# Graph transformer layer, gate logits: full 32-bit products on 32-column weights in place of two-part products on 128 columns

## The reference, cut to what matters

```python
x = x + gnn(xn, ...) + mix(xn, ...)            # attention parts
z = _layernorm(x, axis=-1)                     # (12500, 256)
all_out = _experts_mlp(z, eW1, eb1, eW2, eb2, eW3, eb3)   # 4 experts
shared  = _shared_mlp(z, sW1, sb1, sW2, sb2, sW3, sb3)
gates   = softmax(z @ gW + gb)                 # gW is (256, 4)
topv, topi = top_k(gates, 2)
topw    = softmax(topv)
out     = x + shared + sum(sel(all_out, topi) * topw)
```

## Time and profile before

| what | value |
|---|---|
| median of 3 runs | 1440.02 us (1438.76 to 1440.14) |
| the profiled execution | 1439.86 us, of which the span of the trace is 1438.1 us |
| mean granted TensorE clock | 0.984 |
| PE busy | 1382.2 us (96%) |
| PEld busy | 1244.2 us (87%) |
| DVE busy | 1053.4 us (73%) |
| ACT busy | 769.6 us (54%) |
| POOL busy | 954.6 us (66%) |
| DMA | 121.81 MB, mean 85 GB/s |

### The profile page before, as it was taken

How to read it: one execution, slowest core, us unless ns; L and a number is a source line. 1 busy time by engine, 2 the same in 40 slices (tenths; PEclk the granted TensorE clock), 3 DMA queues, 4 the chain that set the end, 5 groups by cost and what they waited for, 6 DMA issues and landing times.

```text
span 1438.1 us, 26970 instructions
## 1 busy us (share of the span) xinstructions
PE 1382.2 (96%) x9032; PEld 1244.2 (87%) x9032; DVE 1053.4 (73%) x2566; ACT 769.6 (54%) x1339; POOL 954.6 (66%) x873
## 2 busy tenths in 40 slices
PE   5999999679999999999999999999999999999987
PEld 5999999567888888988889888888888888888875
DVE  6877778657777777777778777777777777777761
ACT  4555556125654556545665456554565555655553
POOL 5776766367666776667766677666776666776352
PEclk9999999899999999999999999999999999999998
DMA  5777767222212222121220212202122121220000
GB/s 180 253 261 251 227 207 240 59 66 59 66 30 66 58 72 67 27 65 58 72 68 25 67 55 72 68 25 68 54 72 70 28 64 54 72 72 22 15 15 14
DMA packets 71630, 121.81 MB, mean 85 GB/s; under 512 B 38053, under 2 KB 42786, under 8 KB 71598
## 3 DMA queue, kind: packets, MB, share of 16 engines
q1 hardware_dynamic: 55598, 108.00, 23.6%
q0 software_dynamic: 16000, 13.43, 4.3%
HBM read 69.47 MB, written 51.70 MB: 84 GB/s over the span
## 4 chain that ended last, share of the span: by engine, by line
PE 91%; DVE 3%; POOL 2%; issue 1%; ACT 1%; DVEq 1%; POOLq 1%; DMA 0%; SPq 0%; ACTq 0%
PE psum L224 27%; PE psum L225 26%; PE psum L226 26%; PE psum L421 4%; PE psum L642 1%; PE psum L494 1%; PE psum L573 1%; PE psum L572 1%; PE psum L690 1%; PE psum L566 1%; PE psum L625 1%; PE psum L664 1%; POOL xg L1350 1%; POOL ag L1352 1%; DMA attn_bc<-in_L_gnn_attn_l 0%
## 5 line engine op out<-in xcount | busy, mean ns | idle before, releaser
L224 PE MATMUL psum<-w_hi,h_hi 128*125 128x256 f32 x600 | 171.6, 286 | 4.9 <-DVE h_lo L1236 3.7
L226 PE MATMUL psum<-w_hi,h_lo 128*125 128x256 f32 x600 | 169.3, 282 | 0.0
L225 PE MATMUL psum<-w_lo,h_hi 128*125 128x256 f32 x600 | 169.2, 282 | 0.0
L1350 POOL DMA_INDIRECT xg<-table_xt,idx x100 | 124.6, 1246 | 55.7 <-issue 55.7
L1356 POOL TENSOR_TENSOR h_lo<-relu,h_hi 128x1000 fp32r<-128x1000 f32 x50 | 127.3, 2568 | 29.0 <-ACT h_hi L792 29.0
L1154 DVE SCALAR_TENSOR_TENSOR base<-xb,rn,b_bc 125x256 f32<-125x256 f32 x100 | 144.5, 1485 | 0.3
L1356 POOL TENSOR_TENSOR s_lo<-relu,s_hi 128x1000 fp32r<-128x1000 f32 (+1 forms) x50 | 90.4, 1809 | 77.3 <-ACT s_hi L792 77.3
L1352 POOL DMA_INDIRECT ag<-table_al,idx x100 | 121.0, 1210 | 30.5 <-issue 30.5
L1356 POOL TENSOR_TENSOR e_lo<-relu,e_hi 128x1000 fp32r<-128x1000 f32 x50 | 115.5, 2333 | 17.3 <-DVE scale_rows L1127 15.0
L224 PE MATMUL psum<-xT_hi,w_hi 128*128 128x500 f32 x300 | 120.7, 402 | 1.3 <-ACT h_hi L792 1.3
L224 PE MATMUL psum<-z_hi,w_hi 128*128 128x500 f32 x300 | 119.5, 398 | 2.3 <-DVE z_lo L1185 2.3
(11 more groups left out here) (234 smaller groups left out, 4638.1 us busy)
## 6 DMA issues: line engine op xcount, KB each, us to landing
xb<-in_x SPq DMA_DIRECT2D x50, 448.0 KB
xT_hi_table<-x1T_hi SPq DMA_DIRECT2D x25, 500.0 KB
xT_lo_table<-x1T_lo SPq DMA_DIRECT2D x25, 500.0 KB
xT_hi<-xT_hi_table SPq DMA_DIRECT2D x25, 500.0 KB
xT_lo<-xT_lo_table SPq DMA_DIRECT2D x25, 500.0 KB
table_xt<-xts SPq DMA_DIRECT2D x25, 455.0 KB
out<-xmid SPq DMA_DIRECT2D x25, 448.0 KB
xb<-in_x SPq DMA_DIRECT2D x50, 52.0 KB
```

What stands on the lines that cost most here:

```text
L224: pe.matmul(out, wh, xh, start=first, stop=False)
L225: pe.matmul(out, wh, xl, start=False, stop=False)
L226: return pe.matmul(out, wl, xh, start=False, stop=last)
L1350: pool.indirect_dma_start(xg[par][:, j, :], None, table_xt.ap(), bass.IndirectOffsetOnAxis(idx[par][:, 1, j:j + 1], 0)).then_inc(S[f"gath{ ...
```

## The change

`gate_w` becomes plain 32-bit and 32 columns wide, with the 4 gate weights in the first columns and zeros behind. ScalarE makes one more copy of the transposed features out of banks 0 and 1, `zf` in plain 32-bit (a new semaphore of that name), after `z_lo` is made. `logits_of_z` takes `zf` tile by tile, each tile into a quarter of the partitions of bank 1. `logitsT` is then 125 columns for all four tiles, and one transpose in place of four turns it. VectorE reads 4 columns for each tile, so that the addition of the two partial sums is gone.

```diff
-        gate_w = sb("gate_w", [P, CK, 2, P], F32R)
+        gate_w = sb("gate_w", [P, CK, QUAD])
-        logitsT = sb("logitsT", [P, GR])
+        logitsT = sb("logitsT", [P, R])
+        zf = sb("zf", [P, CK, GR])
...
                 def logits_of_z():
+                    pe.wait_ge(S["zf"], i - 1)
                     for c in range(CK):
-                        pe.matmul(colT(1), gate_w[:, c, 0, :], z_hi[:, c, :], start=c == 0, stop=False)
-                        last = pe.matmul(colT(1), gate_w[:, c, 1, :], z_lo[:, c, :], start=False, stop=c == CK - 1)
+                        for j in range(T):
+                            last = pe.matmul(psum[j * QUAD:(j + 1) * QUAD, 1, 0:R], gate_w[:, c, :], tile(zf, c, j),
+                                             start=c == 0, stop=c == CK - 1)
...
                             pe.wait_ge(S["s1_relu"], 2 * (i - 2) + 1)
-                            for j in range(T):
-                                last = pe.transpose(psum[0:R, 5, j * P:(j + 1) * P], logitsT[:, j * R:(j + 1) * R],
-                                                    ident[:])
-                            last.then_inc(S["lt_mm"], 1)
+                            pe.transpose(psum[0:R, 5, 0:P], logitsT[:], ident[:]).then_inc(S["lt_mm"], 1)
...
                         act.activation(z_hi[:], colT(0, 2), ACT.Copy).then_inc(S["z_hi"], 1)
+                if c:
+                    act.wait_ge(S["zT"], i - 1)
+                    act.activation(zf[:], colT(0, 2), ACT.Copy).then_inc(S["zf"], 1)
...
-                            act.activation(logitsT[:], colT(1), ACT.Copy).then_inc(S["lg"], 1)
+                            act.activation(logitsT[:], psum[:, 1, 0:R], ACT.Copy).then_inc(S["lg"], 1)
...
-                dve.tensor_copy(gate_w[:, :, 0, 0:EXPERTS], gw_raw[:])
-                dve.tensor_copy(gate_w[:, :, 1, EXPERTS:2 * EXPERTS], gw_raw[:])
-                dve.drain()
-                for n, at in ((0, EXPERTS), (1, 0)):
-                    tt(gate_w[:, :, n, at:at + EXPERTS], gw_raw[:], gate_w[:, :, 0, 0:EXPERTS], ALU.subtract)
+                dve.tensor_copy(gate_w[:, :, 0:EXPERTS], gw_raw[:])
...
-                    rows = psum[0:R, 5, :].rearrange("p (j n) -> p j n", j=T)
-                    tt(soft[:, 0, :, :], rows[:, :, EXPERTS:2 * EXPERTS],
+                    rows = psum[0:R, 5, 0:P].rearrange("p (j n) -> p j n", j=T)
+                    tt(soft[:, 0, :, :], rows[:, :, 0:EXPERTS],
                        gb_bc[:].unsqueeze(1).broadcast_to([R, T, EXPERTS]), ALU.add)
-                    dve.drain()
-                    tt(soft[:, 0, :, :], rows[:, :, 0:EXPERTS], soft[:, 0, :, :], ALU.add)
```

More of the change, by code:

```diff
@@ L48 @@
     "w_split1", "xT_free", "xl0", "xl1", "xo0", "xo1", "x0", "x1", "x1T", "x1T_hi", "x1t", "x_split", "xmid", "xn1", "xr_hi",
-    "xr_ones", "xt_mm", "xts", "y", "y0", "y1", "zT", "z_hi", "z_norm", "zeroed", "zt",
[1 row of a table added]
 )
@@ L1302, in _ @@
             pool.memset(ew2_raw, 0.0)
-            pool.memset(gate_w[:].bitcast(F32), 0.0)
+            pool.memset(gate_w[:], 0.0)
             pool.memset(out_bias[:].bitcast(F32), 0.0).then_inc(S["zeroed"], 1)
```

## The result

The changed kernel takes **1428.45 us**, the median of 6 runs (1428.03 to 1429.37), against 1439.63 us of the kernel before, the median of 6 runs (1438.76 to 1440.14). The ratio is 0.9925 with a 95% interval of 0.9913 to 0.9937: 11 us or 0.75% faster. The forecast was 1428.6 us. The profiled execution took 1429.37 us, with a span of 1427.5 us and a mean granted clock of 0.982.

What follows compares the result with a forecast made beforehand. PE, busy throughout each full round, was taken as the bound; 10.8 us from 23 rounds, -0.6 and +0.9 at the ends and +0.3 in setup gave 11.4 us saved, 1428.6 us, with 8-in-10 range 1425.0 to 1435.5.

Steps and rivals of the forecast that it cites:

- What bounds the kernel: Full phase 2 rounds: PE busy for all 44.67 us, so time PE saves in a round is saved 23 times.
- The block, 0.75 us: Logits block: eight 32-bit products cost PE 0.56 + 0.19 us instead of 0.91, saving 0.16 us per round.
- The transposes, 0.31 us: Transposes of `logitsT`: three fewer on PE save 0.31 us per round, 0.21 at the other bound.
- Together 0.47 us per round, 10.8 in all: Block and transposes over 23 full rounds: 10.8 us saved, bounds 8.5 to 13.3.
- The cover: ScalarE in full rounds: `zf` ready 0.6 us before PE wants it, queries 0.3 us to spare, so no cost.
- The ends: Last rounds: round 25 loses 0.6 us waiting for the logits' copy, round 26 gains 0.9.
- The setup, -0.3 us: End of phase 1: less gate-weight preparation on DVE, one cast left, counted as 0.3 us saved.
- The sum: Whole kernel: 10.8 - 0.6 + 0.9 + 0.3 = 11.4 us saved, 1428.6 us against the median of 1440.02.
- The serial passes: Rival, logits block: passes one behind another take 1.8 us, 0.6 us per round worse, 1454 us; chance 0.09 including a longer `zf` wait.

Runs made afterwards that it cites:

- copy_alone: Kernel before plus only a 1000-column ScalarE copy in the place of `zf` and PE's wait for it, old products kept: 1439.99 us, ratio 1.0005.
- four_transposes: Changed kernel with four transposes of `logitsT` instead of one, three repeating the first unread: 1436.86 us, ratio 0.9987.
- queue_push: Changed kernel with one more 1000-column ScalarE activation behind `zf`, copying a buffer onto itself: 1445.65 us, ratio 1.0043.
- both_mended: Changed kernel with three more gate-weight copies on VectorE in phase 1 and the `logitsT` copy ahead of the shared layer's first relu pair: 1426.56 us, ratio 0.9909.
- after_again: Changed kernel unaltered, timed again as the measure for the second group of experiments: 1428.44 us, ratio 0.9923.
- same_quarter: Changed kernel with all four tiles in one partition quarter, loops swapped, 500-column `logitsT` and four transposes: 1467.89 us, ratio 1.0199.
- copy_late: Changed kernel with the `zf` copy and its wait moved behind all four hidden blocks: 1461.01 us, ratio 1.0146.

## Why the prediction was right, point by point

- **What bounds the kernel.** PE back to back in the rounds: right. Each piece taken from PE came back 23 times, and the 1.0 us on ScalarE cost nothing in a full round (copy_alone).
- **The block, 0.75 us.** 0.75 by starts, and 0.18 us saved per round by four_transposes against 0.16. Only its make-up was off: the 0.19 were put behind the block, and half of them lies ahead of it.
- **The transposes, 0.31 us.** 0.33.
- **Together 0.47 us per round, 10.8 in all.** 0.514 and 11.8. The two parts of four_transposes, 0.18 and 0.33, add up to it by construction; the pieces read one by one, 0.91 less 0.75 and 0.44 less 0.11, give 0.49.
- **The cover.** `zf` 0.6 us ahead was forecast, 0.69 measured; the queries 0.3, measured 0.31. queue_push shows its edge: 0.9 us more of push costs 0.72, not nothing.
- **The ends.** In round 25 the experts were to start 0.9 us later. Counted from the matmul ahead of the logits block they start 0.80 us later (2.52 us behind it before, 3.32 now); the trace shows 0.81 us of idle time there, and before there was none. In round 26, again at the lower clock, I put the block at 1.2 us instead of 1.67. It takes 0.99 by starts (1394.88 to 1395.87), and its two neighbours 0.55 and 0.58 instead of 0.42, so 1.28. The wait for the gates fell by 0.37 (3.41 to 3.04), forecast was 0.25. Both ends together were to give 0.3 us, and the stretch behind round 25's block is 0.4 us shorter. Its parts bear the forecast out only where the clock is the same: up to the row transposes of round 26 it is 0.4 us longer (29.64 to 30.02), and from the logits transpose to the gates 0.69 shorter (6.74 to 6.05), where 0.56 was forecast. The 0.4 us of the block itself can't be seen in the time. The stretch from this block to the logits transpose went from 6.19 to only 6.00 us, and in traces of the same work it lies between 4.89 and 6.26 us with the granted clock (0.96 to 0.73).
- **The setup, -0.3 us.** This is the term that failed. The work saved was 0.41 us, but the prediction took it as passed on along the chain. By being earlier VectorE lost its place ahead of GpSimd at the next group, 1.68 us. The net of both is +1.27. The other 0.4 us of the 1.7 come from +1.06 at the start of the kernel (the first `k_lo` at 28.07 instead of 27.01) and -0.66 between the last `k_lo` and the first block (87.10 instead of 87.76). Both are scatter as far as the traces show: over the eleven, the first `k_lo` starts anywhere from 27.01 to 28.34 us, and the latest of all belongs to both_mended, which has the old pace. From the last `k_lo` to the first block the traces have 86.0 to 90.5 us, with 90.47 in after_again, the same kernel.
- **The sum.** 11.4 us less was forecast, and the medians differ by 11.2 us. That the two are so close is luck: between the two spans the rounds gave 1.0 us more than forecast and the setup 2.0 us less, and the profiled execution of the changed kernel happens to be 0.9 us over its median.

The serial passes, the rival on the other side, do not hold for this block, where every quarter works beside the others. In one quarter they do hold as to size: 1.8 us was worked out, 1.82 measured. same_quarter takes 1467.89 us with four transposes; less 23 times 0.33 us for three of them, the change would then have gone to some 1460 us (an estimate). The rival's 1454 us was too low, for the most part because it left out the 0.19 us beside the block, 23 times. The Trainium skill, "FP8 and Floating Point Precision", TensorE Precision Notes, has four passes for such a product. The trace agrees with it as to the time: 0.214 us for 125 columns, where four passes at the rate of the 500-column matmuls come to 0.23. It does not show the passes themselves, since each product has two records, 0.107 us apart.

## What to carry to other kernels

On an engine that is busy all the time, cut work by its distance between starts and add what it costs its neighbours; a new instruction on another engine is free only as far as the nearest reader queued behind it, so work out that slack for each place it could stand, since here 0.3 us was the whole of it and a later place was 2.2% slower. The small weights of 32 columns, in plain 32-bit, paid here only because each tile had a quarter of the partitions of its own. And an engine made faster can fall behind another at a place where the two race, as here in phase 1: compare the starts of the same instruction in before and after, not only the work that was removed.

## What the runs showed of the hardware

The duration of the same VectorE operation depends here on whether GpSimd runs beside it, and on who started first. Over the eleven traces, `kf` of 125x1024 takes 0.69 or 0.70 us if it starts 0.12 to 0.15 us ahead of GpSimd's `xr_lo`, and 2.48 to 2.51 us if it starts 0.24 to 0.27 us behind it, to 0.5 us past the end of that operation (250.04 + 2.20 against 250.30 + 2.48). GpSimd pays in turn: 2.60 to 2.63 us when second, 2.20 when first.

The same thing shows in the rounds, unforecast. The 100 operations `base` of VectorE took in the kernel before, in the changed one, and in copy_late (busy us, mean ns, idle before):

```profile
L1154 DVE SCALAR_TENSOR_TENSOR base<-xb,rn,b_bc 125x256 f32<-125x256 f32 x100 | 144.5, 1485 | 0.3
```
```profile
L1151 DVE SCALAR_TENSOR_TENSOR base<-xb,rn,b_bc 125x256 f32<-125x256 f32 x100 | 93.9, 979 | 0.3
```
```profile
L1151 DVE SCALAR_TENSOR_TENSOR base<-xb,rn,b_bc 125x256 f32<-125x256 f32 x100 | 143.6, 1476 | 0.3
```

Nothing was changed on them. But in the changed kernel the copy on ScalarE delays the third and fourth hidden blocks, and GpSimd pauses 0.79 us between its two `h_lo`:

```profile
693.66 2.60 POOL L1353 TENSOR_TENSOR h_lo<-relu,h_hi 128x1000 fp32r<-128x1000 f32 x1 [1.03 <-ACT h_hi L792]
697.05 2.36 POOL L1353 TENSOR_TENSOR h_lo<-relu,h_hi 128x1000 fp32r<-128x1000 f32 x1 [0.79 <-ACT h_hi L792]
```

VectorE's three `base` of the round then take 3.36 us (693.58 to 696.94) instead of 5.46. The first starts 0.08 us ahead of `h_lo` and takes 0.47 or 0.48 us in both kernels. The second and third, before and after:

```profile
696.47 2.58 DVE L1154 SCALAR_TENSOR_TENSOR base<-xb,rn,b_bc 125x256 f32<-125x256 f32 x1
698.97 2.57 DVE L1154 SCALAR_TENSOR_TENSOR base<-xb,rn,b_bc 125x256 f32<-125x256 f32 x1
```
```profile
693.98 2.57 DVE L1151 SCALAR_TENSOR_TENSOR base<-xb,rn,b_bc 125x256 f32<-125x256 f32 x1
696.47 0.47 DVE L1151 SCALAR_TENSOR_TENSOR base<-xb,rn,b_bc 125x256 f32<-125x256 f32 x1
```

An operation that meets a running `h_lo` ends 0.3 us behind it (693.98 + 2.57 against 693.66 + 2.60), and the one that falls into the pause takes 0.47. In copy_alone, with the old products and the pause, they take 94.1 us in all, and in copy_late, with the new products and GpSimd's two `h_lo` back to back again, 143.6: so it is the pause and not the products. VectorE isn't the bound in the rounds, and its 50 us are worth nothing there. The Trainium skill, "GPSIMD Engine Reference", 1. Specifications, says that GpSimd shares its SBUF interfaces with VectorE, with contention for VectorE's instructions in a two-port mode or with two SBUF inputs. The trace agrees that there is contention, and puts 1.8 us of it on `kf` and 2.1 on one `base`. It shows besides that the operation that starts first keeps its pace and the other one pays.
